# Products of the identity on TensorE in the first stage and the gate logits of a two-layer gated cross-attention and MoE kernel

## The reference, cut to what matters

```python
x = x + tanh(g_xattn[0]) * L0_xattn(ctx, layernorm(x), mask, b)   # 8 heads of 32, 77 keys
x = x + tanh(g_ffn[0]) * L0_ffn(layernorm(x), ...)                # 64 experts, 8 chosen per row, 2 shared
...
def L0_xattn(memory, query, seq_mask, b):
    logits = einsum('bhqd,bhkd->bhqk', Q, K) + b[0] + mask_term
    return einsum('bhqk,bhkd->bhqd', softmax(logits), V)
def route(x, gate_w, gate_bias):
    scores = sigmoid(x @ gate_w.T)          # the gate logits
    ...                                     # choice of groups and experts, weights
```

## Time and profile before

| | us |
|---|---|
| median of three runs | 1510.43 (1507.5 to 1512.0) |
| profiled execution, its own time | 1510.48 |
| its span, first to last instruction | 1508.7 |
| mean granted clock of TensorE | 0.946 of full |
| PE busy | 1351.8 (90%) |
| DVE busy | 858.4 (57%) |
| ACT busy | 700.8 (46%) |
| POOL busy | 544.2 (36%) |

### The profile page before, as it was taken

How to read it: one execution, slowest core, us unless ns; L and a number is a source line. 1 busy time by engine, 2 the same in 40 slices (tenths; PEclk the granted TensorE clock), 3 DMA queues, 4 the chain that set the end, 5 groups by cost and what they waited for, 6 DMA issues and landing times. The chain is left out here.

```text
span 1508.7 us, 31115 instructions
## 1 busy us (share of the span) xinstructions
PE 1351.8 (90%) x8093; PEld 1066.5 (71%) x8093; DVE 858.4 (57%) x2366; ACT 700.8 (46%) x1871; POOL 544.2 (36%) x620
## 2 busy tenths in 40 slices
PE   4989997999999999999446799999998899999998
PEld 3876665777777777777234577676765789999997
DVE  6869982333333333333237467667678576666666
ACT  2443332444444444444124577677776444444443
POOL 1002554333333333333384467666562011111110
PEclk8967998999999999999767899999999999999999
DMA  4025103777666656643441122221120000000000
GB/s 105 0 79 145 33 15 94 213 208 214 204 180 196 192 159 187 203 149 114 119 129 55 50 60 64 57 67 52 44 86 22 15 8 15 15 14 14 14 7 15
DMA packets 107712, 136.14 MB, mean 90 GB/s; under 512 B 29843, under 2 KB 91635, under 8 KB 107603
## 3 DMA queue, kind: packets, MB, share of 16 engines
q1 hardware_dynamic: 64643, 61.15, 13.9%
q0 software_dynamic: 15456, 48.62, 12.0%
q10 hardware_dynamic: 27504, 25.05, 4.9%
HBM read 102.75 MB, written 32.01 MB: 89 GB/s over the span
## 5 line engine op out<-in xcount | busy, mean ns | idle before, releaser
L1259 PE MATMUL ps<-wgu,xT 128*128 (+1 forms) x892 | 310.1, 471 | 2.4 <-ACT xT L1041 1.2
L783 POOL DMA_INDIRECT xg<-n_rows,idx x191 | 181.1, 948 | 295.2 <-DVE wS L2075 208.4
L1259 PE MATMUL ps<-wdn,hT 88*128 (+1 forms) x892 | 228.9, 382 | 2.8 <-DVE hT L2081 1.9
L2235 DVE TENSOR_REDUCE nmx<-ps 128x1 f32<-128x333 f32 x256 | 127.1, 498 | 124.3 <-PE ps L1259 108.6
L1259 PEld LDWEIGHTS ps<-wgu,xT 128*128 128x128 f32 x892 | 155.9, 194 | 54.8 <-issue 6.1
L1137 ACT ACTIVATE pD<-ps,nmx 128x333 f32<-128x333 f32 x256 | 139.2, 546 | 96.7 <-DVE nmx L2235 73.0
L1259 PEld LDWEIGHTS ps<-wdn,hT 88*128 88x128 f32 x892 | 153.7, 191 | 17.5 <-issue 2.7
L2078 DVE TENSOR_TENSOR hC<-sg,ps 128x176 f32<-128x176 f32 x191 | 64.5, 338 | 174.1 <-ACT sg L1092 159.5
L2081 DVE COPY hT<-ps 88x256 f32<-88x256 f32 x191 | 80.3, 420 | 134.1 <-issue 80.8
L1551 PE MATMUL ps<-ident,pD 128*128 128x128 f32 x768 | 131.3, 281 | 27.3 <-DVE pT L2241 16.4
L800 POOL DMA_INDIRECT yg<-y_rows,slotG x128 | 123.2, 963 | 89.8 <-ACT pD L1137 33.4
(11 more groups left out here) (305 smaller groups left out, 3001.2 us busy)
## 6 DMA issues: line engine op xcount, KB each, us to landing
y_rows<-yC ACTq DMA_DIRECT2D x191, 128.0 KB
wgu<-in_wgu SPq DMA_DIRECT2D x64, 352.0 KB
wdn<-in_wdn SPq DMA_DIRECT2D x64, 176.0 KB
xg<-n_rows,idx POOLq DMA_INDIRECT x191
kraw<-in_kD SPq DMA_DIRECT2D x8, 308.0 KB
x<-in_x SPq DMA_DIRECT2D x4, 512.0 KB, 4.9
n_rows<-nB SPq DMA_DIRECT2D x4, 512.0 KB, 3.4
xg<-n_rows SPq DMA_DIRECT2D x16, 128.0 KB, 2.1
```

Of the source, the lines that this page charges most:

```text
L783: pool.indirect_dma_start(out=xg[:, b % XS, :], out_offset=None, in_=n1_rows, in_offset=bass.IndirectOffsetOnAxis(ap=idx[:, b:b + 1], axis ...
L1259: return pe.matmul(o, lhsT, rhs, start=start, stop=stop, **kw)
L2235: dve.tensor_reduce(nmx[:, k:k + 1], ps[:, score_bank(k), 0:NK1], AX, ALU.max, negate=True).then_inc(d_mx, 1)
```

## The change

Nothing is removed. PE gets products of the identity with two copies of itself, 256 columns each, into PSUM columns that no one reads at that time, and in steps 0 and 1 the values of the step are moved ahead of the row transposes of tile t+3:

```diff
+            two_idents = ident[:].unsqueeze(1).broadcast_to([P, 2, P])
+            def keep_busy(bank, n):
+                for _ in range(n):
+                    mm(ps[:, bank, 0:2 * P], ident[:], two_idents, True, True)
-            def a_transpose(t, r):
+            def a_transpose(t, r, fill=0):
+                after(pe, a_nT, t)
+                keep_busy(0, fill)
                 pe.wait_ge(a_n, t + 1)
-                after(pe, a_nT, t)
                 transpose_n(0, r).then_inc(a_t, 1)
...
                 if not (isinstance(t, int) and t + 2 >= NT):
                     a_scores(t + 2, r, i + 1)
-                if not (isinstance(t, int) and t + 3 >= NT):
+                else:
+                    keep_busy(1 + 2 * r, 5)
+                early = isinstance(t, int) and t < 2
+                if not (early or isinstance(t, int) and t + 3 >= NT):
                     a_transpose(t + 3, 1 - r)
                 after(pe, a_od, t)
+                if early:
+                    keep_busy(7, 4)
...
                 last.then_inc(a_o, 1)
+                if early:
+                    a_transpose(t + 3, 1 - r, 8 * t)
+            keep_busy(7, 28)
             a_transpose(0, 0)
...
             a_scores(1, 1, 0)
+            keep_busy(7, 6)
             pe.wait_ge(ld_a, 16 * BATCH)
             pairs(pe, a_step, ahead=4)
+            keep_busy(4, 10)
...
                 last.then_inc(b_l, 1)
+                if t % 2:
+                    keep_busy(4, 1)
```

## The result

The change makes the kernel slower: 1519.77 us (1517.48 to 1522.95) against 1510.43 us (1507.5 to 1512.0), both medians of five runs, a ratio of 1.0058 with the interval 1.0043 to 1.0073. The prediction had 1515.4 us, gave slower a chance of 0.46, and its range ended at 1519.0 us. The profiled execution took 1518.88 us, 8.4 us more than that of before.

The account below looks back on a forecast made before the run. DVE was taken to bound mid-stage, with PE's pace, partly at the lower clock, setting time in a few places. Terms: 4.4 + 2.1 - 0.3 - 1.0 - 0.25 = +4.95 us on 1510.48 us, giving 1515.4 us; range 1508.5 to 1519 us.

Parts of the forecast that it names:

- The price of a product: Each added float32 product on PE takes two passes: 0.435 us at full clock, 0.85 us at the lower level.
- Rival 1: Products of the identity are cheap, one pass each like a transpose; 1507.5 us, faster; chance 13%.
- The start: 28 products ahead of the first transposes end at 18.3 us; the first `sA` comes 4.4 us later, never given back.
- Steps 1 and 2: Four and eight products delay values and scores, so `sA` of tile 4 comes 2.1 us later.
- The bound of +9.8 us: Upper bound for the delay of `sA` of tile 4 behind `sA` of tile 2, with all at the lower level.
- rival 3: The clock stays low: +1.6 us at the start, +3 to 5 us in step 1; 1520 us; chance 10%.
- the signs: Timeline marks for a right forecast, including a 3 to 5 us wait before `sA` of tile 4, `nB` near 105.5 us.
- Steps 2 to 13: DVE bounds them; its small waits for PE just behind 41.06 us go: -0.3 us.
- The stage's end: Steps 14 and 15: five products each keep the clock up; reciprocal of step 15 comes 1.0 us sooner.
- The gate logits: Eighth sigmoid 2 to 3 us sooner after `nB`, mostly lost waiting for the third tile's rows; -0.25 us.
- rival 2: Part of the logits' gain is kept, up to -2 us more; 1513.4 us, no difference; chance 15%.
- The sum: Terms from the start to the gate logits add to +4.95 us, giving 1515.4 us, 0.33% slower.

Follow-up runs that it names:

- start_only: The kernel before with only the 28 products ahead of the first transposes; ratio 1.0015 to the kernel before.
- twelve_first: The change with step 1's eight products moved ahead of the values, twelve in one piece; one run, first gather at 240.70 us.
- order_only: The kernel before without products, only values of steps 0 and 1 moved ahead of the row transposes; ratio 0.9992 to the kernel before.
- old_steps: The change with steps 0 and 1 as before: no four or eight products, old order; ratio 1.0028 to the kernel before.
- end_only: The kernel before with only the products of steps 14 and 15, behind them and in the gate logits; ratio 0.9977 to the kernel before.
- rows_end: end_only, with SP loading the third tile's shared-expert rows between the fifth and sixth expert's weights; ratio 0.9969 to the kernel before.
- rows_before: The kernel before with only SP's third-tile row load moved between the fifth and sixth expert's weights; ratio 1.0002 to the kernel before.
- hold: The change without step 1's four and eight products, but eleven ahead of its wait for `a_od`; ratio 0.9988 to the kernel before.
- best: hold with 12 instead of 28 products at the start; ratio 0.9951 to the kernel before.
- rows_best: best, with SP loading the third tile's rows between the fifth and sixth expert's weights; ratio 0.9945 to the kernel before.

## Why the prediction was right or wrong

**The price of a product: right.** The 20 passes behind step 15 lasted from 107.79 to 112.19 us, 0.44 us a product at full clock (0.435 forecast). At the lower level eight passes lasted 37.28 to 40.85 us, 0.89 us a product (0.85). Rival 1, one pass a product, is out: 28 products show 56 passes. So is the formula of the Trainium skill for this case (TensorE: Matmul & The Clock Gate, Back-to-back issue gap): an estimate by it is 3.1 us for 28 products, and the trace has 14.8 us.

**The start: right.** First transposes at 18.71 us (18.3), first `sA` +4.7 us (+4.4), and start_only shows that nothing gives it back.

**Steps 1 and 2: the step that failed.** The path was as forecast: PE idle until `a_od`, level down, products in the way of the values and then of the scores. The size was not: +2.1 us forecast, +7.5 us measured. The term went wrong at one choice: "I take 2.8 us, with the level back during them". The level wasn't back behind the four products, nor behind the values that follow them, but only towards the end of the eight. So the four took 3.57 us and not 2.8, the values 3.3 us and not 1.86, and the eight 6.5 us and not 3.5. These three sum to 5.2 of the 5.4 us that are missing; the other 0.2 us lie between the last of the eight and `sA` (2.57 us instead of 2.33). The row that stood against my choice was shown: at the start the level rose 3.5 to 5.4 us after PE had begun, longer than the 1.7 to 3.4 us of the four products. I used this interval for the 28 products and not for the four. twelve_first shows the cause: the same twelve products in one piece cost 3.9 us less, with the level back in time for the values; order_only and old_steps show that neither the moved order nor the late start costs anything there. The bound of +9.8 us held the truth, but the forecast's own range allowed the level only 2 us in step 1, and rival 3, the low clock, had only 10%. Its 1520 us is where the time came out, in part by luck: its low clock in step 1 came true with more than its 3 to 5 us, its late rise at the start (+1.6 us) did not, and 1 us more came back in the logits than either counted on. Of the signs, the first transposes, `sA` of tile 2 and the level at the stage's end (1.00 from 54 to 125 us) came as forecast; the wait before `sA` of tile 4 (7.2 us, not 3 to 5) and the first `nB` (111.24 us, not 105.5) did not.

**Steps 2 to 13: right.** From `sA` of tile 4 to that of tile 15 it is 43.3 us instead of 43.6 us, -0.3 us as forecast.

**The stage's end: right.** -1.2 us against -1.0 us, and end_only has it too.

**The gate logits: the mechanism right, the size too small.** The choice came 2.2 us sooner after `nB`, and 1.7 us of it were lost in front of the third tile's rows, as forecast; from `nB` to the first gather 1.3 us were given back instead of 0.25 us: 0.5 us because the rows landed a little sooner, 0.6 us between them and `places()`, where the lower level ended sooner (rival 2, in part), and 0.2 us behind it. rows_end and rows_before show the link.

**The sum.** 4.7 + 7.5 - 0.3 - 1.2 - 1.3 = 9.4 us; measured 9.3 us at the first gather and 9.3 us in the medians.

## What to carry to other kernels

Work that only keeps a clock up must stand where its engine would stand anyway, ahead of the wait and not behind it, and last as long as the wait: longer, it delays what follows (28 products at the start), shorter, it leaves a gap (hold and best against rows_best). Count it at the lower level unless the stretch ahead of it is shown to be at the full one, and take a rise within a piece only where the trace has one behind a piece as short. A gain early in a chain can be lost at the next wait: look for what the freed engine waits for next (here a load behind the weights of eight experts in one queue), and move that as well.

## What the runs showed of the hardware

Busy is not the same as at full clock. In the change PE was busy without a gap from 37.3 us on and had 0.50 up to 50 us; what stood between its two blocks of products were the values, 16 passes of 33 columns in 3.3 us. In twelve_first, with the blocks in one piece ahead of the values, the stretch from 41 to 44 us had 0.97. These two differ only in the order (and in the PSUM bank that the eight write); which property of the values matters, no run separates. Nor do such passes bring the level down: from 54 to 95 us of the change PE did values, transposes and scores without a gap at 1.00. The gate logits were the other way round in the kernel before, busy without a gap and at 0.50:

```profile
103.00:112.00 9.00, 9.00 (x49) 9.00 (x48) 3.70 (x13) 5.25 (x16) 0.00 (x0) 0.50 0.92 300
```

In the change, with one product more for every two tiles, they began at 1.00 and kept it.

At the lower level a pass of 256 columns took 0.446 us in step 1 (eight in 3.57 us), 5% over what the score passes of 308 columns at the start lead one to expect (0.426 us); I didn't look for the cause.
